# Two copies of x for a graph network's prologue: features on partitions for the own product, the split's scale from a sum of squares

## The reference

```
edge_index = jnp.stack([src, dst])
x = _layernorm(x + _L0_gnn_ref(x, src, dst, edge_attr_128, W, b_W, W_e, b_We))
x = _layernorm(x + _L1_gnn_ref(x, edge_index, W1, b1, gamma, beta))
```

## Time and profile before

| | |
|---|---|
| median of 3 runs | 937.04 us (936.41 to 938.98) |
| the profiled execution: its own time | 937.3 us |
| its span | 935.2 us |
| PE busy, share of the span | 884.7 us, 95% |
| DVE busy | 675.8 us, 72% |
| ACT busy | 463.2 us, 50% |
| first matmul of block 0's counts | 21.71 us |
| start of the last low split | 61.20 us |

### The profile page before, as it was taken

The page is one execution under the profiler, slowest core; times in us unless marked ns, Lnnn a source line. Parts: engine busy times, 40 slices in busy tenths (PEclk is TensorE's granted clock), DMA queues, the critical chain, the costliest instruction groups (busy, mean ns, idle before and its releaser), DMA issues.

```text
span 935.2 us, 30524 instructions
## 1 busy us (share of the span) xinstructions
PE 884.7 (95%) x12210; PEld 791.8 (85%) x12210; DVE 675.8 (72%) x1248; ACT 463.2 (50%) x1008; POOL 350.1 (37%) x401
## 2 busy tenths in 40 slices
PE   4868999999999999999999999999999999999995
PEld 4757888888988898989999999999988888888874
DVE  6899899999999998898888899888841111112245
ACT  3764666656666666556565556565542000000036
POOL 2236444455554444455334455334332011112200
PEclk9988999999999999999999999999999999999998
DMA  6327999898878788776777658678667897779644
GB/s 179 110 81 296 365 341 336 305 334 293 308 268 303 284 311 274 235 247 224 253 264 276 220 184 305 222 267 284 204 217 301 344 356 278 273 259 326 249 154 136
DMA packets 96762, 244.77 MB, mean 262 GB/s; under 512 B 39560, under 2 KB 64838, under 8 KB 90726
## 3 DMA queue, kind: packets, MB, share of 16 engines
q1 hardware_dynamic: 95014, 239.46, 72.4%
q0 software_dynamic: 1600, 3.28, 1.4%
HBM read 183.85 MB, written 58.85 MB: 260 GB/s over the span
## 4 chain that ended last, share of the span: by engine, by line
PE 85%; DVE 5%; issue 3%; ACT 3%; DMA 1%; SPq 1%; ACTq 0%; DVEq 0%
PE x_ps L876 26%; PE pair_ps L951 18%; PE pair_ps L858 13%; PE e_ps L895 10%; PE x_ps L884 9%; PE j_ps L933 2%; PE j_ps L981 2%; DVE lo_oh L616 1%; DVE key_oh L619 1%; PE pair_ps L960 1%; PE j_ps L934 1%; PE u_vps L1409 1%; ACT counts L1065 1%; PE u_vps L1417 1%; DMA counts_kept<-counts 1%
## 5 line engine op out<-in xcount | busy, mean ns | idle before, releaser
L1065 ACT CAST counts<-pair_ps 128x784 bf16<-128x784 f32 x391 | 315.3, 817 | 252.4 <-PE pair_ps L858 246.4
L876 PE MATMUL x_ps<-counts,xsplit 128*128 128x256 bf16 (+1 forms) x2450 | 307.8, 271 | 0.0
L616 DVE TENSOR_TENSOR lo_oh<-counter,lo_t 128x2048 bf16<-128x2048 bf16 x196 | 252.9, 1290 | 54.4 <-PE pair_ps L858 53.3
L876 PEld LDWEIGHTS x_ps<-counts,xsplit 128*128 128x128 f16 x2450 | 222.3, 98 | 29.4 <-issue 7.1
L858 PE MATMUL pair_ps<-key_oh,lo_oh 128*128 128x100 bf16 x3128 | 208.3, 209 | 22.7 <-ACT counts L1065 14.4
L858 PEld LDWEIGHTS pair_ps<-key_oh,lo_oh 128*128 128x128 bf16 x3128 | 182.8, 98 | 37.4 <-issue 20.0
L619 DVE TENSOR_TENSOR key_oh<-counter,key_t 128x1600 bf16<-128x1600 bf16 x196 | 196.3, 1002 | 0.0
L895 PE MATMUL e_ps<-streams 128*32 128x128 f32 x3528 | 107.0, 274 | 0.3 <-issue 0.3
L884 PE MATMUL x_ps<-counts,zown 128*128 128x256 bf16 (+1 forms) x840 | 105.8, 269 | 0.0
L951 PE MATMUL pair_ps<-streams,zown 128*128 128x256 bf16 x878 | 99.0, 273 | 0.0
L895 PEld LDWEIGHTS e_ps<-streams 128*32 128x32 f32 x3528 | 93.5, 110 | 4.9 <-issue 1.0
(11 more groups left out here) (181 smaller groups left out, 889.7 us busy)
## 6 DMA issues: line engine op xcount, KB each, us to landing
streams<-in_edge_attr SPq DMA_DIRECT2D x196, 576.0 KB, 9.8
counts_kept<-counts SPq DMA_DIRECT2D x10, 1600.0 KB, 8.7
streams<-counts_kept SPq DMA_DIRECT2D x6, 1600.0 KB, 6.5
counts<-counts_kept SPq DMA_DIRECT2D x4, 1600.0 KB, 7.1
counts_kept<-counts SPq DMA_DIRECT2D x2, 3136.0 KB, 12.4
streams<-counts_kept SPq DMA_DIRECT2D x2, 3136.0 KB, 14.8
edst<-in_dst SPq DMA_DIRECT2D x196, 4.5 KB
streams<-in_x SPq DMA_DIRECT2D x3, 1024.0 KB, 5.7
```

Source lines behind the costliest of these rows:

```text
L616: dv.tensor_tensor(lo_oh[:, ring, :, :, :].rearrange("p r w k t -> p (r w) k t"), counter[:, :, :].unsqueeze(1).to_broadcast([P, g, P, 2]) ...
L876: last = nc.tensor.matmul(x_ps[:, 0, 0:n], xsplit[:, q // 2, q % 2, :], by_hi[:, q // 2, :], start=(q == 0), stop=(q == 2 * HS - 1))
L1065: a.copy(out.rearrange("p h (g n) -> p h g n", g=2), pair_ps[at % 2][:, :, 0:4 * KW].rearrange("p g (n h) -> p h g n", h=HI)[:, 0:HS]).the ...
```

## The change

The host lays x out twice as a kernel input: `x_rows`, as it stood in SBUF before, and `x_columns`, with features on partitions. `x_columns` is loaded straight into `zown`, where `own_product` takes each tile as it is and `own_out` writes the result over it. So the turns and their copies on ACT go, and own products alternate between two PSUM buffers (`j_ps`, `e_ps`).

The scale comes from the sum of all squares of x. `sum_squares` multiplies each tile of `x_columns` with itself on PE, all 49 into one PSUM tile; its diagonal is taken and summed on DVE (`add_squares`), summed over partitions by one PE pass against a matrix of ones, and made into the scale on all partitions by five small instructions (`scales`). The row maxima are taken later, from `xsplit` (in blocks 16, 18 and 20).

The prologue is reordered: all four row loads and the weights are issued ahead of x; the search for the starts of blocks 2 and 3, and the second weights' preparation, come ahead of block 0; the three high splits and the first two low splits stand one slot earlier, the last low split stays in slot 4 of block 1.

```diff
-LARGEST_AT = (None, 2, 4)
-TOP_AT, SCALES_AT, SPREAD_AT = 5, 8, 12
-HIGH_AT, LOW_AT = (11, 13, 15), (16, 18, 20)
+NORM_AT, TOTAL_AT, SCALES_AT = 7, 8, 11
+HIGH_AT, LOW_AT = (10, 12, 14), (15, 17, 20)
+ROWS_CHECKED_AT = (16, 18, 20)
+SQUARED_IN = ((4, 5, 6), (7, 8), (9, 10), (11, 12))
...
-            for b in range(2):
+            for b in range(ROW_RING):
                 load_rows(sp, b)
             sp.dma_start(wi, W0[:, 0:F]).then_inc(S["wi_in"], 16)
-            load_inputs(sp, {"x": xf}, x, S, range(1))
-            for b in range(2, ROW_RING):
-                load_rows(sp, b)
             load_weights(sp, {"wj": wj, "we": we, "bi": bi, "bj": bje, "be": be_t[:, :]}, W0, b0, We, be, S)
+            load_pieces(sp, columns, x_columns, S["columns_in"], range(1))
             sp.wait_ge(win_in[0], 32)
-            load_inputs(sp, {"x": xf}, x, S, range(1, len(X_PIECES)))
+            load_pieces(sp, columns, x_columns, S["columns_in"], range(1, len(X_PIECES)))
+            load_pieces(sp, xf, x_rows, S["x_in"], range(len(X_PIECES)))
...
+            def add_squares():
+                dve.wait_ge(S["squares_summed"], 1)
+                step(dv.tensor_tensor(x1_mem[:, 0, :], squares_ps, ident[:, :], ALU.mult))
+                dv.tensor_reduce(out=norm[:, :], in_=x1_mem[:, 0, :], axis=AX.X, op=ALU.add).then_inc(S["norm_ready"], 1)
+
+            def scales():
+                dve.wait_ge(S["norm_out"], 1)
+                step(dv.tensor_copy(top[:, :], norm_ps))
...
+            def row_largest(k):
                 at = piece_tiles(k)
-                dve.wait_ge(S["x_in"][k], 16 * x_loads(k))
-                last = dv.tensor_reduce(out=rowmax[:, at], in_=xrows[:, at, :], axis=AX.X,
-                                        op=ALU.max, apply_absolute_value=True)
+                step(dv.tensor_reduce(out=rowmax[:, at], in_=xsplit[:, at, 0, :], axis=AX.X,
+                                      op=ALU.max, apply_absolute_value=True))
...
+                    if s == 7 and b in ROWS_CHECKED_AT:
+                        row_largest(ROWS_CHECKED_AT.index(b))
...
-                    if b == 1 and s == 6:
-                        ready_weights()
...
+            def sum_squares(m):
+                columns_here(m)
+                h, n = OWN[m]
+                for k in range(h, h + n):
+                    last = nc.tensor.matmul(squares_ps, own[:, k, :], own[:, k, :], start=(k == 0), stop=(k == HS - 1))
+                last.then_inc(S["columns_squared"], 1)
...
             def own_product(m):
                 h, n = OWN[m]
+                columns_here(m)
                 pe.wait_ge(S["weights_ready"], 1)
-                pe.wait_ge(S["xT_out"], m + 1)
-                reach(pe, S["own_added"], m)
+                reach(pe, S["own_added"], m - 1)
                 for k in range(n):
-                    last = nc.tensor.matmul(j_ps[:, k, :], xT[m % 2][:, k, :], wi,
-                                            start=True, stop=True)
+                    last = nc.tensor.matmul(own_ps[m % 2][:, k, :], own[:, h + k, :], wi, start=True, stop=True)
                 last.then_inc(S["own_done"], 1)
 
-            for b in range(2):
+            for b in range(ROW_RING):
                 find_rows(b)
             for m in range(OWN_FIRST):
-                turn_x(m)
-                if m >= 1:
-                    own_product(m - 1)
+                sum_squares(m)
+                own_product(m)
             turn_keys(0)
-            for b in range(2, 4):
-                find_rows(b)
-            own_product(OWN_FIRST - 1)
             pe.wait_ge(S["starts_known"], 2)
...
+                        if s < len(SQUARED_IN):
+                            for m in SQUARED_IN[s]:
+                                sum_squares(m)
+                        if s == TOTAL_AT:
+                            pe.wait_ge(S["norm_ready"], 1)
+                            nc.tensor.matmul(norm_ps, ones[:, :], norm[:, :], start=True, stop=True).then_inc(S["norm_out"], 1)
+                        if s >= 1 and OWN_FIRST + s - 1 < len(OWN):
                             own_product(OWN_FIRST + s - 1)
-                        if OWN_FIRST + s < len(OWN):
-                            turn_x(OWN_FIRST + s)
```

More of the change, by code:

```diff
@@ L169, in all_turns, with load_pieces @@
             step(i)
-def load_inputs(sp, t, x, S, pieces):
-    full = x[0:(NB - 1) * BN, :].rearrange("(b p t) f -> p b (t f)", p=P, t=2)
+def load_pieces(sp, out, table, loaded, pieces):
     for k in pieces:
[L175 to L185, removed]
+        at = piece_tiles(k)
+        sp.dma_start(out[:, at.start * F:at.stop * F], table[:, at.start * F:at.stop * F]).then_inc(loaded[k], 16)
 def load_weights(sp, t, W0, b0, We, be, S):
@@ L291, in layers @@
         S["x_in"] = [sem(f"x_in{k}") for k in range(len(X_PIECES))]
+        S["columns_in"] = [sem(f"columns_in{k}") for k in range(len(X_PIECES))]
         win_in, edst_in, e_in = two("window_in"), two("edge_dst_in"), two("edges_in")
@@ L753, in _ @@
                 start_of(b)
+            dv.memset(total[:, :], 0.0)
+            step(dv.tensor_copy(ebase[:, :], ebase_i[:, :]))
+            ready_weights()
+            make_keys(0)
             for b in range(NB + 2):
@@ L961, in weights, with columns_here @@
                   .then_inc(S["projected"], 1)
-            def turn_x(m):
+            def columns_here(m):
                 h, n = OWN[m]
-                piece = [h < 2 * z for _, z in X_PIECES].index(True)
-                last_piece = [h + n <= 2 * z for _, z in X_PIECES].index(True)
-                for k in range(piece, last_piece + 1):
-                    pe.wait_ge(S["x_in"][k], 16 * x_loads(k))
-                pe.wait_ge(S["consts"], CONSTS)
-                reach(pe, S["xT_out"], m - 1)
-                for k in range(n):
-                    last = nc.tensor.transpose(turn_ps[m % 2][:, k, :], xrows[:, h + k, :], ident[:, :])
-                last.then_inc(S["x_turned"], 1)
+                first, last = ([end <= 2 * z for _, z in X_PIECES].index(True) for end in (h + 1, h + n))
+                for k in range(first, last + 1):
+                    pe.wait_ge(S["columns_in"][k], 16)
@@ L1141, in own_out @@
                 act.wait_ge(S["own_done"], m + 1)
[L1142 removed]
+                reach(act, S["columns_squared"], m + 1)
+                a.copy(own[:, h:h + n, :], own_ps[m % 2][:, 0:n, :]).then_inc(S["own_added"], 1)
             def float_rows(b):
@@ L1796, with x_layouts @@
         "L1_gnn_W", "L1_gnn_b", "L1_gnn_gamma", "L1_gnn_beta"]
+def x_layouts(np, x):
+    tiles = np.zeros((HS, P, F), x.dtype)
+    whole = (NB - 1) * BN
+    tiles[0:HS - 1] = x[0:whole].reshape(NB - 1, P, 2, F).transpose(0, 2, 1, 3).reshape(HS - 1, P, F)
+    for half in range(2):
+        tiles[HS - 1, 64 * half:64 * half + LAST_P] = x[whole:].reshape(LAST_P, 2, F)[:, half]
+    return [np.ascontiguousarray(tiles.transpose(order)).reshape(P, HS * F) for order in ((1, 0, 2), (2, 0, 1))]
 def kernel(**inputs):
```

131 lines of the change are left out of this document (47 added, 84 removed).

## The result

The changed kernel takes 946.17 us (median of 4 runs, 944.26 to 947.69) where the kernel before, run beside it, takes 936.72 (4 runs, 936.32 to 938.98). It is slower by about 9.5 us; the ratio on record is 1.0095, with a 95% interval of 1.008 to 1.0109 (the two medians alone would give 1.0101). Forecast were 5.0, and the range reached to 946.5. The profiled execution took 947.1 us (span 945.3), 10.1 more in span than before.

A forecast was written before the change was run, and what follows sets the result against it. It took the end of the last low split as the clock of the start: 2.8 us later at the first count, 3.0 at the scale, 5.0 at that split, so 937.3 + 5.0 = 942.3 us; 8-in-10 range 936.5 to 946.5.

The forecast's parts named there:

- SP's list: SP's fixed work (edges, start values, destinations) from the last low split's end to the store of counts: 12.0 us, unchanged.
- late columns: Case at the start: the column piece takes 8.5 us, sum 2.8 larger, 945; chance 0.17 together with uncovered maxima.
- uncovered maxima: Case that the row maxima in blocks 16, 18 and 20 show, up to 6.9 us; chance 0.17 together with late columns.
- Columns landed at 11.2: Start of x: first column piece issued near 5.5, landing 5.7 us later, so PE begins at 11.2 instead of 7.92.
- 64 passes in 9.95 us, first count 3.35 later: PE ahead of block 0: squares and own products end at 21.15, first count near 24.5; start 2.8 us later.
- 21.2 us from the first count to the total's pass, 3.9 at the lower level: PE in block 0: 19.3 us of passes plus 1.95 for 3.9 us at the lower clock; total there at 46.0.
- the clock stays at its upper level: Rival at the start: clock holds over PE's 3.1 us gap, 1.95 us go, 940.3 alone; smaller loss has chance 0.20.
- Total to the end of the last low split 22.6: DVE in blocks 0 and 1: from total at 46.0 to last low split's end at 68.6, 22.6 us.
- The store lands after 11.5: Ahead of block 2: the store of block 0's counts takes 11.5 us from issue to landing, unchanged.
- ACT's copy near 92.2: At block 2's start: ACT's copy begins near 92.2 instead of 87.24, the stall ending 5.0 us later.
- Behind it nothing: After the stall at block 2: no further gain or loss, row maxima in blocks 16, 18 and 20 taken as 0.
- DVE was the bound, and the change frees it: Rival in block 0: DVE loses 4.9 us of maxima, 932.4; break-even with the total at 41.1; chance 0.15.

The follow-up runs named there:

- e3: Changed kernel with the store of block 0's counts issued by SP ahead of the wait for the low splits: 939.61 us, ratio 1.0029.
- e4: Kernel before the change with the same single edit on SP, block 0's counts stored ahead of the wait for the low splits: 933.76 us, ratio 0.997.
- e5: Changed kernel with the first column piece of x issued ahead of the five second weights: 940.15 us, ratio 1.0039.
- e12: The changed kernel itself, measured again without any edit: 945.29 us, ratio 1.0102.
- e1: Changed kernel with the scale made at slot 12, behind the one-hots of slots 12 and 13: 945.42 us, ratio 1.009.
- e7: Changed kernel with the scale at slot 12 as in e1, and low splits at slots 16, 18 and 20: 941.98 us, ratio 1.0052.
- e6: Changed kernel with squares and own products of groups 2 and 3, and their ACT copies, behind block 0's keys: 941.73 us, ratio 1.0044.
- e9: Changed kernel without the three row maxima of blocks 16, 18 and 20 and the row check they feed: 944.64 us, ratio 1.0094.
- e2: Changed kernel with the sum of squares over 13 of 49 tiles, so the scale rests on part of x: 937.31 us, ratio 1.0017.
- e11: Kernel before the change with only the row loads and the search for blocks 2 and 3 put first: 932.82 us, ratio 0.9954.
- e8: Changed kernel with the edits of e3, e5, e6 and e7 together: 927.7 us, ratio 0.9884.

## Why the prediction was right, and where its terms were off

The sign and the mechanism held: more passes on PE and a later start move the total, the total moves the low splits, these move SP's store, and the store moves block 2. One thing in it was too narrow: the store is not needed for the loss. PE itself reached block 2 5.6 us later, and with the store out of the way in both kernels (e3, e4) 5.85 us remained. The size was off, 10.1 us in span against 5.0. Of the 5.1 that were missing, about 1.6 had arisen by the end of the last low split (70.2 instead of 68.6), 1.9 in SP's list, 0.3 in the store and 1.4 behind it. That 946.2 still lies in the range, by 0.3 us, is in part luck: the upper end was there for late columns and uncovered maxima, while SP's list was taken as fixed in every case. The terms are these.

*Columns landed at 11.2.* They landed at 13.2, 7.8 us after the issue at 5.44: **2.0 us mis-sized.** Of the two ends, 4.0 and 8.5, the slow one was nearer. The fit of the Trainium skill (DMA: Bandwidth & Descriptors, "Anatomy of one DMA"), which it gives for DMAs on GpSimd's path, makes an estimate of 4.4 us for this piece. e5's profile, where it is issued by SP at 3.07 and PE starts on it at 8.28, has at most 5.2, and the changed kernel's 7.8 is far above either. Why the later issue takes longer stays open.

*64 passes in 9.95 us, first count 3.35 later.* 9.8 and 3.4: right, by two errors that cancel. The last 40 passes took 0.112 us each, not 0.122, and the slow pace of the first ones lasted 5.3 us, not 4.

*21.2 us from the first count to the total's pass, 3.9 at the lower level.* 20.8 to the pass, 21.1 to its end at 47.5, in the profile; the lower level held for 5.7 us instead, and the faster passes paid for it. In e12, where it didn't fall, DVE reads the total 18.45 us behind the first count (25.48 to 43.93). So e12 is the rival "the clock stays at its upper level" come true, with the total 2 us ahead of the forecast's 46.0, and it took 944.9 us where that rival had 940.3: the clock was not what the forecast lacked.

*Total to scale 0.9.* It was 0.8.

*Total to the end of the last low split 22.6.* It was 22.7, but the reason, that the pair of slots 12 and 13 now stands on DVE's way and costs 2.0, is refuted as put by e1: the first low split waits for ACT's high split, so the pair ahead of it is free, or worth at most 0.7 us. What costs 1.7 us here, and 2.4 by the usual 21.3, is that the first low split now stands ahead of a pair that could fill that wait, as e7 shows with both moved. By those six profiles the whole stretch is 23.3 to 23.4 us, so the 22.7 that fits the forecast so well is a short case.

*SP's list 12.0 us.* From the end of the last low split to the store it was 13.85: **1.9 us mis-sized.** The chain has an issue of edges of 1.53 us in it among others of 0.33 (start, duration, what), and SP's own rows show 4.63 us for the eight destinations, which took 3.85 before (the last three rows shown are of the kernel before):

```profile
70.92 1.53 SPq L328
...
72.63 0.33 SPq L328
```

```profile
73.52 0.47 SPq L289 DMA_DIRECT2D rows_i<-in_dst  x1
78.94 4.63 SPq L320 DMA_DIRECT2D edst<-in_dst  x8
83.61 0.43 SPq L356 DMA_DIRECT2D dinv_rows<-dinv  x1
84.09 0.43 SPq L335 DMA_DIRECT2D counts_kept<-counts  x1
```

```profile
65.79 0.51 SPq L301 DMA_DIRECT2D rows_i<-in_dst  x1
71.27 3.85 SPq L333 DMA_DIRECT2D edst<-in_dst  x8
...
75.65 1.70 SPq L349 DMA_DIRECT2D counts_kept<-counts  x1
```

So 1.2 of the 1.9 us are among the edges (70.24 to 73.52, before 63.67 to 65.79) and 0.8 among the destinations.

From the start of that split to the store it was 14.45 us before and 16.1 to 17.0 in six profiles of this order (e1, e5, e6, e7, e9, e12), though only 14.85 in e2, and 15.47 in e11, which has the DVE order of before. That the list itself depends on when it runs was not in the sum, and what makes it longer stays open.

*The store lands after 11.5.* 11.9. *ACT's copy near 92.2.* 95.99 here and 92.81 in e12. *Behind it nothing.* 1.4 us more were lost behind the copy in the profiled execution (10.1 in span against 8.75), 2.3 in e12 and 0.3 to 2.4 in the other profiles of this order. It comes ahead of the row maxima, which run only from 472 us on: PE's waits from 100 to 400 us are 8.8 us in all, 7.1 before, and the one that grew stands ahead of the sums of edge features (total, times, longest; now, then before):

```profile
PE e_ps L873 <- issue: 2.9, 3, 2.0
```

```profile
PE e_ps L895 <- issue: 0.3, 1, 0.3
```

What PE waits for there the profile doesn't name. On the maxima the forecast was right (e9).

*Of the rivals,* "DVE was the bound, and the change frees it" is refuted: DVE loses the maxima ahead of the scale (2.29 and 2.41 make 4.7 us in block 0, not 4.9) and waits for PE. Its break-even, the total at 41.1, was put too late: e5 has its total at 39.07 and is 0.39% slower than before still, e2 at 37.77 is level with it. Against the forecast's terms, e5 loses 0.8 us between the total and the last low split, 1.8 in SP's list and 2.4 behind the copy; in e2 these are 0.8, 0.4 and 0.6.

## What to carry to other kernels

When the bound engine is given new work, here 98 passes to spare another engine a few us, ask where on the path it lands, and what it stands ahead of; the same kernel with its start and one store reordered gained 1.2% where it had lost 1%. That is no proof that the new algorithm pays: the old one has gained by reordering too (2.1 us in e4, 4.7 in e11), and with both of these edits together, near 930.5 us by an estimate that takes both gains off 937.3, it was not run against e8's 927.7. A stall that can be traced to one late store is cheap to remove, but what it gives back is only the distance to the next wait, here 2 us in one kernel and 6 in the other. A change that bundles a reorder with a new algorithm should be timed in its parts: here one part of the reorder alone gained 4.7 us inside a change that lost 9.5.

## What the hardware showed that was not expected

The clock doesn't answer the same gap the same way. In the changed kernel run again (e12) the gap of PE is again 3.15 us, and the clock stays up:

```profile
25.48 0.53 PE L834 MATMUL pair_ps<-key_oh,lo_oh 128*128 128x100 bf16 x8 [3.15 <-DVE key_oh L604]
25.84 2.90 PE L951 MATMUL x_ps<-zown 128*128 128x128 f32 x24
```

```profile
25.00:26.00 1.00, 0.52 (x9) 1.00 0.99 417
26.00:28.00 2.00, 2.00 (x20) 1.00 0.97 374
```

The same 24 passes took 5.35 us in the changed kernel's first profile, some 4.5 in e1, e3 and e9, and 2.90 in e5, e7 and e12, all behind an idle gap of PE just like it. In e1, e3 and e9 the clock was still at 1.00 when PE took up its work, fell 1.1 to 1.4 us behind the first count, and was back by 30.2; e1's rows:

```profile
25.00:26.00 1.00, 0.78 (x12) 1.00 1.00 422
26.00:27.00 1.00, 1.00 (x9) 0.67 0.99 418
27.00:28.00 1.00, 1.00 (x7) 0.50 0.96 372
```

The fall makes these 24 passes up to 2.5 us longer, which is likely a part of the spread between runs (944.3 to 947.7). What decides it no run here shows. The printed clock is not the whole account either: at the start of the squares, from 13.25 to 18.52, PE took 0.22 us a pass, as at 0.50, while the clock's row prints 1.00 throughout, and only then 0.112.
